# Perceiver block on one core: u and c loaded from ScalarE's queue, last pair's rows kept on chip, Wr turned between the gates' tiles, first c loaded by itself

## The reference, cut to what matters

```
x1 = x + xattn(layernorm(x), ctx)
xn = layernorm(x1)
z  = sigmoid(xn @ Wg.T + bg)
for t in range(64):                       # h: 32 sequences x 512
    pred = h @ Wr.T + br
    h = df * h + (1 - df) * z[:, t] * (xn[:, t] - pred)      # df = sigmoid(decay)
    y[:, t] = h
x2 = x1 + (layernorm(y) * ln_w + ln_b) @ Wo.T + bo
x3 = x2 + experts(layernorm(x2))
```

## Time and profile before

| | us |
|---|---|
| median of 3 runs | 1320.73 (1319.16 to 1321.11) |
| the profiled execution | 1317.1 |
| its span in the profile | 1315.4 |
| granted TensorE clock, mean | 0.975 |

### The profile page before, as it was taken

The page is one execution under the profiler, slowest core; times in us unless marked ns, Lnnn a source line. Parts: engine busy times, 40 slices in busy tenths (PEclk is TensorE's granted clock), DMA queues, the critical chain, the costliest instruction groups (busy, mean ns, idle before and its releaser), DMA issues. The chain is left out here.

```text
span 1315.4 us, 29577 instructions
## 1 busy us (share of the span) xinstructions
PE 1212.2 (92%) x10417; PEld 727.2 (55%) x10418; DVE 733.1 (56%) x1573; ACT 410.2 (31%) x888; POOL 589.0 (45%) x642
## 2 busy tenths in 40 slices
PE   0799999999999999999979699998599999999993
PEld 0444444444444444444367456665488888888883
DVE  4555667555566755555379667888623223232235
ACT  2334445443444543344155111112211111111110
POOL 1033332223333222333059567787396663530972
PEclk9999999999999999999989899998799999999997
DMA  8545664444566444466074578852223444412556
GB/s 279 222 171 211 217 216 156 164 158 172 212 215 215 148 170 156 172 217 208 9 234 140 165 248 283 289 194 97 65 66 142 159 151 151 158 49 71 152 168 185
DMA packets 99377, 225.45 MB, mean 171 GB/s; under 512 B 14153, under 2 KB 30665, under 8 KB 95217
## 3 DMA queue, kind: packets, MB, share of 16 engines
q1 hardware_dynamic: 87872, 189.46, 42.0%
q0 software_dynamic: 10288, 33.57, 7.5%
q10 hardware_dynamic: 1152, 1.57, 0.5%
HBM read 179.21 MB, written 45.35 MB: 171 GB/s over the span
## 5 line engine op out<-in xcount | busy, mean ns | idle before, releaser
L325 POOL TENSOR_TENSOR wb<-wb,w 128x512 f32<-128x512 f32 x120 | 149.3, 1276 | 337.3 <-ACT wb L508 337.3
L395 PE MATMUL S<-ctxT,x 32*64 32x416 f32 (+1 forms) x4096 | 185.6, 512 | 15.9 <-DVE ctxT L636 15.9
L395 PEld LDWEIGHTS S<-ctxT,x 32*64 32x64 f32 x4096 | 108.9, 133 | 94.0 <-issue 45.0
L618 DVE STREAM_TRANSPOSE ctxT<-ctx_one 128x1024 f32<-128x1024 f32 (+1 forms) x128 | 115.0, 947 | 22.7 <-DMA ctx_one<-in_ctx_dram 22.6
L430 PE MATMUL O<-ctx_one,probsT 128*64 128x512 f32 (+1 forms) x448 | 110.7, 610 | 0.0
L522 ACT ACTIVATE x<-S,w2R,w3R 128x128 f32<-128x128 f32 x256 | 93.4, 491 | 19.2 <-PE S L386 19.2
L1949 POOL TENSOR_TENSOR w_low<-w_low,w_high 128x2048 fp32r<-128x2048 f32 x21 | 96.7, 4607 | 1.7
L2134 DVE TENSOR_TENSOR f_hL<-f_TH,f_hH 128x512 fp32r<-128x512 f32 x39 | 27.0, 692 | 120.4 <-ACT f_hH L2087 120.4
L2092 ACT ACTIVATE sg<-f_G 128x512 f32<-128x512 f32 x39 | 23.3, 597 | 193.5 <-PE f_G L2034 193.5
L508 ACT ACTIVATE wb<-w,hcb 128x512 f32<-128x512 f32 x120 | 77.6, 747 | 0.0
L1465 PE MATMUL Pb<-WrT,yT 128*32 128x128 f32 x2016 | 68.7, 277 | 8.5 <-DVE yT L1725 8.0
(11 more groups left out here) (286 smaller groups left out, 2481.6 us busy)
## 6 DMA issues: line engine op xcount, KB each, us to landing
ctx_one<-in_ctx_dram SPq DMA_DIRECT2D x64, 512.0 KB, 4.5
x<-in_ctx_dram SPq DMA_DIRECT2D x16, 1536.0 KB
ctx_two<-in_ctx_dram SPq DMA_DIRECT2D x16, 1536.0 KB, 9.4
ctx_one<-in_ctx_dram SPq DMA_DIRECT2D x64, 256.0 KB, 5.2
w_low<-_L_ffn_gate_up_proj_dram POOLq DMA_DIRECT2D x10, 1024.0 KB, 8.0
f_xt<-routed_x SPq DMA_DIRECT2D x39, 256.0 KB, 2.7
routed_y<-f_yt SPq DMA_DIRECT2D x39, 256.0 KB, 2.0
w_low<-_L_ffn_gate_up_proj_dram SPq DMA_DIRECT2D x6, 1024.0 KB, 8.5
```

What stands on the lines that cost most here:

```text
L325: pool.tensor_tensor(wb[:, slot, b], wb[:, slot, b], w0[:, c], ALU.add).then_inc(wb_ready, 1)
L395: last = pe.matmul(S[64 * b:64 * b + 64, a, 0:tiles * Q], qr[a * Q:(a + 1) * Q, k, 64 * b:64 * b + 64], ctxT[a * Q:(a + 1) * Q, 0:tiles, b ...
L618: return dve.transpose(ctxT[:, pos:pos + n, b], src[:, i:i + n, :].rearrange("p t (k r) -> p t k r", r=Q))
```

## The change

The last pair's sum is written to the sixteenth tile of `x2` itself, where the gates read it: SP's load of x1 for the gates leaves this tile out, and the wait for its store moves to the end of SP's stream in the gates. Wr's blocks are permuted by ACT at the end of its steps 10 to 13 and copied to WrT at the end of its steps 12 to 15; PE turns one behind each of the products of tiles 11 to 14, into four banks of their own (`WR`). DVE scales block 0 of Wo at the end of the gates, block 1 at the start of the recurrence. In the recurrence SP loads c of tile 0 first, under a semaphore of its own (`c_first`), then u; ACT issues u and c for tile k + 2 at the end of its tile k. SP now issues `load_x(k)` and then `load_ahead(k)`, which waits for the states before tile k only.

```diff
@@ cross_attention, SP and DVE
             sp.wait_ge(x1_ready, PAIRS)
-            sp.dma_start(x1[PAIRS - 1], xb[1][:]).then_inc(x1_out, 16)
-            sp.wait_ge(x1_out, 16 * PAIRS)
+            sp.dma_start(x1[PAIRS - 1], x2[:, PAIRS - 1, :]).then_inc(x1_last, 16)
+            sp.wait_ge(x1_out, 16 * (PAIRS - 1))
...
+                rows = x2[:, PAIRS - 1, :] if step == "last" else xb[s][:]
                 dve.wait_ge(y_done, p + 1)
-                dve.tensor_tensor(xb[s][:], Y[:], xb[s][:], ALU.add).then_inc(x1_ready, 1)
+                dve.tensor_tensor(rows, Y[:], xb[s][:], ALU.add).then_inc(x1_ready, 1)
@@ recurrence_gates, SP
-            sp.dma_start(xt[:, END:TILES, :], x1[END:TILES].rearrange("k p d -> p k d")).then_inc(x_end, 16)
+            sp.dma_start(xt[:, END:TILES - 1, :], x1[END:TILES - 1].rearrange("k p d -> p k d")).then_inc(x_end, 16)
...
+            sp.wait_ge(x1_last, 16)
@@ recurrence_gates, PE
+            def turn_wr(n):
+                pe.wait_ge(wr_permuted, n + 1)
+                for q in range(C):
+                    last = pe.transpose(WR[n][:, q * P:(q + 1) * P], rw.w_perm[n % 2][:, q, :], ident[:])
+                last.then_inc(wr_full, 1)
-            with pe.Fori(0, TILES // 2 - 1) as i:
+            with pe.Fori(0, TILES // 2 - 3) as i:
...
+            for n in range(C):
+                k = TILES - C + n
+                turn(k, k % 2)
+                gates(k - 1, (k - 1) % 2)
+                turn_wr(n)
             gates(TILES - 1, 1)
-            pe.wait_ge(xnL_ready, TILES)
-            for n in range(C):
-                pe.wait_ge(wr_permuted, n + 1)
-                if n >= 2:
-                    pe.wait_ge(wr_ready, n - 1)
-                for c in range(C):
-                    last = pe.transpose(T[n % 2][:, c * P:(c + 1) * P], rw.w_perm[n % 2][:, c, :], ident[:])
-                last.then_inc(wr_full, 1)
@@ recurrence_gates, ACT
+            def permute_wr(n):
+                act.wait_ge(rw.loaded, rw.all_loaded)
+                if n >= 2:
+                    act.wait_ge(wr_full, n - 1)
+                act.copy(rw.permuted_into(n), rw.permuted(rw.Wr[:, n])).then_inc(wr_permuted, 1)
+            def take_wr(n):
+                act.wait_ge(wr_full, n + 1)
+                act.copy(rw.WrT[:, :, n * P:(n + 1) * P], WR[n][:].rearrange("p (c e) -> p c e", c=C)).then_inc(wr_ready, 1)
+            early = TILES - C - 2
...
-            for k in (TILES - 2, TILES - 1):
+            for k in range(early, TILES):
                 step(k, k % 2)
+                if k - early < C:
+                    permute_wr(k - early)
+                if k - early >= 2:
+                    take_wr(k - early - 2)
             gate(TILES - 1, 1)
-            for n in range(C):
-                act.wait_ge(wr_full, n + 1)
-                act.copy(rw.WrT[:, :, n * P:(n + 1) * P], T[n % 2][:].rearrange("p (c e) -> p c e", c=C)).then_inc(wr_ready, 1)
+            act.wait_ge(wr_ready, C)
@@ recurrence_gates, DVE
             for k in (TILES - 2, TILES - 1):
                 u_product(k, k % 2, k // 2)
-                permute_wr(k - TILES + 3)
-            permute_wr(3)
+            dve.wait_ge(rw.loaded, rw.all_loaded)
+            dve.wait_ge(wr_full, C - 1)
+            rw.scale_bo(dve, 0)
+            rw.scale_wo(dve, 0)
@@ recurrence, SP
-            load_uc(0, 0)
-            load_uc(1, 1)
+            sp.dma_start(ct[0][:], c_d[:, 0:ST, :]).then_inc(c_first, 16)
+            sp.dma_start(ut[0][:], u_d[:, 0:ST, :]).then_inc(uc_in[0], 16)
+            load_uc(sp, 1, 1)
...
                 if k == 0:
                     sp.wait_ge(zero_set, 1)
+                else:
+                    sp.wait_ge(h_ready, ST * k)
...
                 load_x(cur, s)
-                if more:
-                    sp.wait_ge(h_ready, ST * k + ST)
-                    load_uc(nxt, s)
@@ recurrence, ACT, at the end of body(k)
+                if k + 2 < TILES:
+                    act.wait_ge(h_ready, ST * k + ST)
+                    load_uc(act, k + 2, n % 2)
@@ recurrence, DVE
-            for k in range(2):
-                if k:
-                    dve.wait_ge(w_permuted, k)
-                scale_bo(k)
-                scale_wo(k)
+            dve.wait_ge(w_permuted, 1)
+            rw.scale_bo(dve, 1)
+            rw.scale_wo(dve, 1)
...
-                if st == 0:
-                    dve.wait_ge(uc_in[s], 32 * loads)
+                if first(k):
+                    dve.wait_ge(*((uc_in[s], uc_loaded(s, loads)) if st else (c_first, 16)))
+                elif st == 0:
+                    dve.wait_ge(uc_in[s], uc_loaded(s, loads))
```

More of the change, by code:

```diff
@@ L726, in body @@
                 if back:
-                    add_x(p, s)
+                    add_x(p, s, step)
             def second_factor(p, s, step):
@@ L780, in __init__, with permuted, permuted_into, scale_bo @@
         self.all_loaded = 16 * len(self.transfers)
-    def permuted(self, n, src):
-        r = self.decay.shape[0] // 4
-        return self.w_perm[n % 2][:].rearrange("p q (c r) -> p q c r", r=r), src.rearrange("p (c q r) -> p q c r", q=4, r=r)
+    def permuted(self, src):
+        return src.rearrange("p (c q r) -> p q c r", q=4, r=self.decay.shape[0] // 4)
+    def permuted_into(self, n):
+        return self.w_perm[n % 2][:].rearrange("p q (c r) -> p q c r", r=self.decay.shape[0] // 4)
+    def scale_bo(self, dve, k):
+        dve.tensor_tensor_reduce(out=self.w_scaled[:], in0=self.Wo[:, k], in1=self.ln_b[:], scale=1.0, scalar=0.0,
+                                 op0=ALU.mult, op1=ALU.add, accum_out=self.bo_col[:, k:k + 1]).then_inc(self.bo_step, 1)
+    def scale_wo(self, dve, k):
+        dve.wait_ge(self.bo_step, k + 1)
+        dve.tensor_tensor_reduce(out=self.w_scaled[:], in0=self.Wo[:, k], in1=self.ln_w[:], scale=1.0, scalar=0.0,
+                                 op0=ALU.mult, op1=ALU.add, accum_out=self.w_sum[:, k:k + 1]).then_inc(self.wo_step, 1)
+        dve.wait_ge(self.wo_step, 2 * k + 1)
+        dve.tensor_scalar(self.w_nmean[:, k:k + 1], self.w_sum[:, k:k + 1], -1.0 / self.ln_w.shape[1], None, ALU.mult).then_inc(self.wo_step, 1)
+        dve.wait_ge(self.wo_step, 2 * k + 2)
+        if k >= 2:
+            dve.wait_ge(self.wo_full, k - 1)
+        dve.tensor_scalar(self.permuted_into(k), self.permuted(self.w_scaled[:]), self.w_nmean[:, k:k + 1], None, ALU.add).then_inc(self.w_permuted, 1)
     def load(self, eng):
@@ L804, in load, with recurrence_gates @@
             eng.dma_start(dst, src).then_inc(done, 16)
-def recurrence_gates(nc, sh, ident, x1, bg, br, decay, u_d, c_d, rw, rt, ahead):
+def recurrence_gates(nc, sh, ident, x1, x1_last, bg, br, decay, u_d, c_d, rw, rt, ahead):
     D, C, N = sh.D, sh.C, sh.N
@@ L837, in recurrence_gates @@
         WT = T + Z
+        WR = [stack.enter_context(nc.psum_tensor(f"g_W{n}", [P, 512], F32)) for n in range(C)]
         row_in = sem("g_row_in")
@@ L1278, in walk, with uc_loaded @@
                 body(k, k % RING, False, None)
+        def uc_loaded(s, loads):
+            return 32 * loads - (16 if s == 0 else 0)
         def scattered(k, loads):
@@ L1414, in body @@
                         if st == 0:
-                            pool.wait_ge(uc_in[s], 32 * loads)
+                            pool.wait_ge(uc_in[s], uc_loaded(s, loads))
                         if st == 1 and has(k - 5):
@@ L2284, in program @@
             rw = RecurrenceWeights(nc, sh, Wr, Wo, decay, ln_w, ln_b, bo, gate_w, inner)
-            recurrence_gates(nc, sh, ident, x1, bg, br, decay, u_d, c_d, rw, rt, ahead)
+            recurrence_gates(nc, sh, ident, x1, x1_last, bg, br, decay, u_d, c_d, rw, rt, ahead)
             recurrence(nc, sh, ident, x1, u_d, c_d, rw, rt, ex)
```

69 lines of the change are left out of this document (25 added, 44 removed).

## The result

The changed kernel takes 1310.88 us (median of 6 runs, 1308.39 to 1314.22) against 1320.23 of the kernel before on the same chip (6 runs, 1319.16 to 1321.11): a ratio of 0.9922, interval 0.9902 to 0.9941, so faster by 9.4 us. The profiled execution took 1311.46; its part ahead of the gates happened to be 1.25 us longer than in the profile of before, and its part behind the last state 1.65 us longer (414.12 against 412.47). The edits are read from what lies between.

The account below looks back on a forecast made before the run. Bound by waits at the borders into the gates and the recurrence, and by GpSimd's waits for x in the scan. 3.9 (1.6 from the first border) - 1.8 + 5.8 = 7.9 us, so 1320.7 - 7.9 = 1312.8, range 1309.5 to 1316.

Parts of the forecast that it names:

- first border: Border from context attention into the gates: no wait for the last x1 store, 1.6 us gained (bounds 0 and 1.7).
- gates' start to second state: From the gates' first statistics to the scan's second state: with the first border's 1.6, 3.9 us earlier in all.
- the clock behind it: Scan's start: TensorE idles, two more predictions at the low clock plus 0.5 for Wo, 1.8 us lost (bounds 0, 4.4).
- tiles 3 to 15: Scan's tiles: GpSimd's waits for x vanish, 5.8 us gained (bounds 0 and 5.8).
- absolute mark of 660.0: Sign at the border into the gates: first statistics near 660.0 us in the profile, before 661.63.
- Wr inside the gates: Gates, tiles 10 to 15: Wr's copies and turns stand beside other work; last c 0.2 us later (bounds 0, 0.6).
- Start of the scan: Recurrence start: c loaded first, Wo set 0 scaled earlier; H's copy at 735.3 instead of 738.25, prediction 0.69 behind.
- third turn of Wo: Scan's start, within the clock loss: this turn stands ahead of one prediction and costs 0.5 us.
- ScalarE's queue: Scan: ScalarE issues u and c after its norm, 1.85 us after the state; landings of 3.0 to 5.5, cover 8.2.
- slower rival: Scan: u and c late behind the weight, landing beyond 8.2 us; 17 us lost, 7.9 won, 1329.9; chance 0.05.
- The scan: Tiles 3 to 12 took 5.8 us excess, blamed on x issued right behind an expert weight on SP; all regained.
- first rival: Scan: x wait stays since x's quarter of DMA engines may have work left; 5.8 not gained, 1318.6; chance 0.14.

Follow-up runs that it names:

- wait_last_store: Changed kernel with SP waiting again for the last store of x1 before the gates; 1312.92 us, ratio 0.9931.
- wr_behind: Changed kernel with Wr turned behind the last gate product again, permuted by DVE; 1309.62 us, ratio 0.9912.
- queue_only: Kernel before with only the scan's queue edits: u and c from ScalarE, x ahead of padding and weight on SP; 1312.68 us, ratio 0.9949.
- undo_queue: Changed kernel with its scan queue part undone: SP issues u and c, then padding and weight, as before; 1318.6 us, ratio 0.9997.
- sp_new_order: Changed kernel, new order kept, but SP issues u and c itself, behind x, padding and weight; 1310.73 us, ratio 0.9934.
- act_old_order: Changed kernel, u and c still from ScalarE, but padding and weight back at the tile's end, just ahead of the next x; 1312.74 us, ratio 0.9949.
- after_again: The changed kernel run once more with no edit; 1310.94 us, ratio 0.9924.
- after_x_split: Changed kernel with each x load cut into four DMAs of 32 rows; 1309.01 us, ratio 0.9911.
- x_on_act: Changed kernel with x of each tile issued by ScalarE at the tile's start instead of SP; 1312.9 us, ratio 0.9947.

## Why the prediction was right

The forecast was 1312.8, the measured median 1310.88. By its steps, in the two profiles, from the last add of the context attention to the last state (before 657.63 to 902.64, after 658.88 to 895.29):

| step | predicted us | measured us |
|---|---|---|
| first border | 1.6 | 1.63 |
| gates' start to second state | 2.3 | 2.35 |
| the clock behind it | -1.8 | -1.03 |
| tiles 3 to 15 | 5.8 | 5.65 |
| sum | 7.9 | 8.60 |

- **First border.** Right, and alone shown by wait_last_store. The absolute mark of 660.0 was not met (661.25), since the part ahead of it was longer in that execution; the distance to the add was.
- **Wr inside the gates.** Predicted 0.2 later for the last c, in the profile 0.19 sooner. The sign can't be read: from the first statistics to the last c store it is 69.37 to 70.74 us in the four executions with Wr behind the gates (wr_behind 69.37), 69.79 to 70.87 in the ten with Wr between the tiles. The prediction never gave the move a gain, and wr_behind shows 0.3 us at most.
- **Start of the scan.** H's copy was to come 75.3 us behind the first statistics (735.3 - 660.0) and came 74.97 behind. The prediction behind it starts 0.63 later, said was 0.69. With the border that is 3.98 us for the second state; 3.9 was said. Part of that closeness is luck: from the first statistics to the second state, the three with the old start took 80.35, 79.95 and 81.33, and eight with the new one and no filling 78.00 to 79.20 (mean 78.80), so that over all the term is nearer 1.7 than 2.3. How it divides between c as the first load and the set of Wo scaled earlier no run shows, since the two were never run apart.
- **The clock.** Two more slow predictions than before were counted, at 0.63 each. In the first profile one more came whole and a little of another (1.94, 1.94 and 1.16 against 1.71, 1.08 and 1.08), so fewer but dearer ones: 1.94 instead of 1.71, as in every execution of the new start without filling. The 0.5 for a third turn of Wo was not needed. The term is 1.03 to the end of tile 2 in the first profile, and 1.08 to 1.60 up to the fifth state over nine executions of the new start without filling (7.89 to 8.41 against 6.81). Not all of it is the change's: with the old start queue_only took 8.66 there. So it was sized somewhat high, and part of it is chance.
- **ScalarE's queue.** ScalarE issues u 0.96 behind the state, sooner than the 1.85 taken. The condition of the slower rival, a landing of c beyond 8.2 us, was nearer than I thought: the median went from 4.2 to 6.0 and the longest from 5.5 to 7.2. It did not decide.
- **The scan.** 5.8 was said for the whole of the excess, and the first profile shows 5.65. But the cause was only half seen, and part of that closeness is luck. The order is what does it when u and c stay on SP (15.5 to 2.9 us of waits, undo_queue against sp_new_order); yet the same order, with x unsplit and issued by SP, gives anything from 1.4 to 10.4 us of waits, and 100.42 to 105.24 us for tiles 3 to 12. The prediction's "nothing large stands ahead of x for a whole tile" does not hold: the weight of the tile before is issued 7.6 us ahead of x and lands after 10.3 to 14.6 in the median of these executions. The first rival, that a quarter of the engines could have work left when x comes, is true in part of the executions; I had put it at 0.14 as a whole, where it acts as a share. That ScalarE's queue gives most of the gain without the order (act_old_order) was in no rival. In the medians the scan's part is larger than the 5.8 said, 6.7 us (queue_only against the kernel before) or 7.9 (sp_new_order against undo_queue).

The gain of 9.35 us in the medians is no sum of these steps. The two profiled executions differ by 5.64 us, the 8.60 less what the changed kernel's lost ahead and behind (1.25 and 1.65); the part behind the last state alone runs from 412.1 to 414.1 us over all fourteen profiles. And the profiled execution of the kernel before is 3.1 us faster than its median, that of the changed kernel 0.6 slower; where a median execution of the kernel before loses its 3.1, no trace shows.

## What to carry to other kernels

A large load that is not urgent goes behind the small one that the next step needs, a whole stage ahead of its successor, and not into the gap just before it; look at how many DMA engines the small one uses, since splitting it so that it uses all can take away the waits that its place leaves. Compare the times of issue, not the queues: here a large load on another queue was in the way just as much. Where two conditions end within a few tenths of each other, moving one of them gives nothing until the other moves too. A wait taken out on the path just ahead of TensorE's work can return part of its worth as a lower clock; products whose results nobody reads kept the clock up here, and must not stand ahead of the work that is waited for.

## What the runs showed of the hardware

- The 256 KB load of x moves 85 to 101 GB/s at a share of 0.26 when it is nearly alone. Cut into four DMAs of 32 rows, with the same bytes, it left the waits for it at none and brought the median landing of a 1 MB weight beside it from 12.6 to 6.9 us (after_again, after_x_split), the weight being issued 3.7 us behind the first piece instead of 2.3 behind x.
- The landing of one and the same weight load, in the same place of the program, has a median of 10.6, 12.6 and 14.6 us in three executions (the changed kernel twice, and wait_last_store), and 8.4 us where x is issued right behind it.
- With a weight issued 2.1 to 2.2 us ahead of x on average, it made no measurable difference whether both stood in one queue or in two (act_old_order 1312.74 us, x_on_act 1312.9).
- At the 1.2 GHz level the 32 small products of a prediction take 1.94 us, at 2.4 GHz 1.08; the 1.71 of the kernel before lay between, in a stretch that averaged 0.63.
